# A transposing transfer in place of TensorE turns for the features of a graph-attention layer

## The reference, cut to what matters

```python
def _gat_layer(h, mask, b):
    scores = jnp.einsum('...nd,...md->...nm', h, h)
    scores = jnp.where(mask, scores, NEG)
    attn = jax.nn.softmax(scores, axis=-1)
    return jnp.einsum('...nm,...md->...nd', attn, h) + b
...
h = jnp.einsum('bnc,hdc->bhnd', x, Wh)
out_h = _gat_layer(h, mask[None, None], bh[None, :, None, :])
...
h2 = jnp.einsum('bnk,dk->bnd', z, Wo)
out2 = _gat_layer(h2, mask[None], bo)
```

## Time and profile before

| | us |
|---|---|
| median of 3 runs (lowest, highest) | 1996.86 (1995.81, 1998.15) |
| the profiled execution | 1996.86 |
| its span in the profile | 1995.1 |
| PE matmul busy | 1904.9 (95%) |
| DVE busy | 1623.2 (81%) |
| ACT busy | 1243.6 (62%) |
| POOL busy | 1013.7 (51%) |
| FA transfers, 640 of 64 KB, issue to landing | 2.0 (median) |

### The profile page before, as it was taken

How to read it: one execution, slowest core, us unless ns; L and a number is a source line. 1 busy time by engine, 2 the same in 40 slices (tenths; PEclk the granted TensorE clock), 3 DMA queues, 4 the chain that set the end, 5 groups by cost and what they waited for, 6 DMA issues and landing times.

```text
span 1995.1 us, 95063 instructions
## 1 busy us (share of the span) xinstructions
PE 1904.9 (95%) x43624; PEld 1563.2 (78%) x43624; DVE 1623.2 (81%) x1975; ACT 1243.6 (62%) x1886; POOL 1013.7 (51%) x742
## 2 busy tenths in 40 slices
PE   8998899999999999999999999999999999989998
PEld 6787799977777777777777777777777777767887
DVE  6999999567787878778787878788778877767998
ACT  5887676246666666666666666666666666654342
POOL 6676899432345444444544444553445454253653
PEclk7999999999999999999999999999999999999999
DMA  7000000011111111111111111111111111101111
GB/s 182 4 4 4 3 2 3 2 34 35 35 34 34 32 33 33 30 35 34 35 35 32 35 28 35 33 34 35 34 34 29 34 31 33 35 13 25 25 25 35
DMA packets 88255, 61.24 MB, mean 31 GB/s; under 512 B 45616, under 2 KB 86832, under 8 KB 87856
## 3 DMA queue, kind: packets, MB, share of 16 engines
q1 hardware_dynamic: 85632, 54.57, 11.2%
q10 hardware_dynamic: 2224, 0.59, 0.1%
HBM read 8.98 MB, written 4.19 MB: 7 GB/s over the span
## 4 chain that ended last, share of the span: by engine, by line
PE 69%; DVE 15%; ACT 5%; POOL 5%; issue 2%; DMA 2%; SPq 1%; ACTq 0%; POOLq 0%; DVEq 0%
PE ACC L1638 29%; PE S L1819 22%; PE S L1798 8%; DVE ring L1412 6%; PE AX L1862 3%; DVE ring L1266 2%; PE AX L1871 2%; PE AX L1839 2%; POOL sp_log L788 1%; POOL ln_sq L791 1%; DMA FA<-lo 1%; ACT ring L1066 1%; PE AX L1618 1%; DVE score L1421 1%; PE S L1695 1%
## 5 line engine op out<-in xcount | busy, mean ns | idle before, releaser
L1638 PEld LDWEIGHTS ACC<-V,ring 128*64 128x64 f32 x28672 | 953.5, 138 | 180.5 <-DVE ring L1266 34.0
L1412 DVE TENSOR_TENSOR ring<-ring,mask_self_t 128x1024 f32<-128x1024 f32 x640 | 822.1, 1287 | 270.0 <-ACT ring L1066 261.3
L1638 PE MATMUL ACC<-V,ring 128*64 128x65 f32 x28672 | 972.6, 223 | 29.7 <-DVE ring L1266 12.3
L1066 ACT ACTIVATE ring<-S,dot_bias 128x1024 f32<-128x1024 f32 x640 | 713.4, 1115 | 420.3 <-PE S L1819 384.4
L1819 PE MATMUL S<-FA 128*64 128x512 f16 x5120 | 666.5, 382 | 7.5 <-DMA FA<-lo 7.5
L1819 PEld LDWEIGHTS S<-FA 128*64 128x64 f16 x5120 | 253.3, 110 | 168.6 <-ACT ring L1066 15.9
L1266 DVE SCALAR_TENSOR_TENSOR ring<-S,pair_q,mask_t 128x1024 f32<-128x1024 f32 x256 | 315.1, 1272 | 15.1 <-DVE f_max L1278 4.6
L804 POOL TENSOR_TENSOR EV_both<-score,recip 128x512 f32<-128x512 f32 x64 | 115.4, 1803 | 222.3 <-DVE score L1421 222.2
L797 POOL TENSOR_TENSOR V<-v_pairs,bh_bc 128x512 f32<-128x512 f32 x64 | 95.4, 1490 | 164.9 <-ACT v_pairs L1086 164.9
L1798 PE MATMUL S<-parts,mask_t 128*128 128x128 bf16 x3072 | 172.0, 219 | 1.6 <-DVE o L1401 1.4
L1798 PEld LDWEIGHTS S<-parts,mask_t 128*128 128x128 bf16 x3072 | 171.6, 98 | 1.8 <-issue 1.8
(11 more groups left out here) (134 smaller groups left out, 2078.9 us busy)
## 6 DMA issues: line engine op xcount, KB each, us to landing
FA<-hi SPq DMA_DIRECT2D x320, 64.0 KB, 2.0
FA<-lo SPq DMA_DIRECT2D x320, 64.0 KB, 2.0
X<-in_x SPq DMA_DIRECT2D x16, 256.0 KB, 5.0
ring<-in_adj SPq DMA_DIRECT2D x8, 512.0 KB, 8.4
out_x<-X SPq DMA_DIRECT2D x16, 256.0 KB, 2.6
wh<-in_wh_t ACTq DMA_DIRECT2D x2, 64.0 KB, 6.5
bh_bc<-in_bh ACTq DMA_DIRECT2D x1, 128.0 KB, 9.7
w_gat<-in_w_gat ACTq DMA_DIRECT2D x4, 16.0 KB, 3.7
```

The source lines that it names most:

```text
L1066: act.activation(ring[:, jt, :], S[jt % 2][:, :], ACT.Exp, bias=dot_bias[:, n % 2:n % 2 + 1])\
L1412: dve.tensor_tensor(ring[:, jt, :], ring[:, jt, :], mask_self_t[:, jt, :], ALU.mult)\
L1638: last = pe.matmul(acc_of(t)[rows, :], ring[:, jt, t * P + c * CUT:t * P + (c + 1) * CUT], values, start=(jt == 0 and t % 4 == 0), stop=(j ...
```

## The change

The features are no longer turned by PE. ACT copies the high half straight from `v_pairs` (SBUF) into a new buffer HL, node-major: for each node 64 high and 64 low values side by side. DVE makes the low half from `v_pairs` and HL. SP then issues one transposing transfer of the whole of HL's buffer (128 partitions x 1024 columns) into FA[:, par, 0], waits for it (`stacked`), and issues two plain copies of 128 KB that exchange the halves into FA[:, par, 1]. The step "F" leaves the order of the AX banks. Heads 0 and 1 are turned after tile 7 of head 3 instead of tile 5 on PE, and copied after tile 7 instead of 6 on ACT. ACT waits for the low half of the unit before (`lo_made`) before it writes `v_pairs` anew, and for the transfer out of the same HL buffer before it writes there. In the last layer the rest of the last unit is made after tile 3, ahead of its norms, and not after tile 5.

```diff
-        hi = sb("hi", [P, 2, HALF], F16)
-        lo = sb("lo", [P, 2, HALF], F16)
+        HL = sb("HL", [P, 2, T, 2 * D], F16)
...
+        stacked = [sem("stacked0"), sem("stacked1")]
...
         def moved_by(u):
-            return 16 * 8 * (u["n"] // 2 + 1)
+            return 16 * 2 * (u["n"] // 2 + 1)
...
             for u in UNITS:
                 par = buf_of(u)
-                moved = features_in[par]
-                sp.wait_ge(hi_made, u["n"] + 1)
-                for half in range(2):
-                    cols_of = slice(half * HALF, (half + 1) * HALF)
-                    own = slice(half * D, (half + 1) * D)
-                    sp.dma_start(FA[0:D, par, 0, cols_of], hi[own, par, :]).then_inc(moved, 16)
-                    sp.dma_start(FA[D:P, par, 1, cols_of], hi[own, par, :]).then_inc(moved, 16)
                 sp.wait_ge(lo_made, u["n"] + 1)
-                for half in range(2):
-                    cols_of = slice(half * HALF, (half + 1) * HALF)
-                    own = slice(half * D, (half + 1) * D)
-                    sp.dma_start(FA[D:P, par, 0, cols_of], lo[own, par, :]).then_inc(moved, 16)
-                    sp.dma_start(FA[0:D, par, 1, cols_of], lo[own, par, :]).then_inc(moved, 16)
+                sp.dma_start_transpose(out=FA[:, par, 0, :].rearrange("p (t n) -> p t n", t=T),
+                                       in_=HL[:, par, :, :].rearrange("p t n -> p (t n)")).then_inc(stacked[par], 16)
+                sp.wait_ge(stacked[par], 16 * (u["n"] // 2 + 1))
+                sp.dma_start(FA[0:D, par, 1, :], FA[D:P, par, 0, :]).then_inc(features_in[par], 16)
+                sp.dma_start(FA[D:P, par, 1, :], FA[0:D, par, 0, :]).then_inc(features_in[par], 16)
...
                 wait(act, v_made, u["n"])
+                wait(act, lo_made, u["n"])
                 act.activation(v_pairs, V_FULL, ACT.Copy).then_inc(v_copied, 1)
...
             def features(u):
-                k, at = AX_AT["F", u["n"]]
-                act.wait_ge(ax_full[k], at + 1)
                 if u["n"] >= 2:
-                    act.wait_ge(features_in[buf_of(u)], moved_by(UNITS[u["n"] - 2]))
-                act.activation(hi[:, buf_of(u), :], AX[k][:, :], ACT.Copy).then_inc(hi_made, 1)
+                    act.wait_ge(stacked[buf_of(u)], 16 * (u["n"] // 2))
+                act.activation(halves_of(HL[:, buf_of(u), :, 0:D]), v_pairs, ACT.Copy).then_inc(hi_made, 1)
...
-                if jt == 6 and is_head(u, 3):
+                if jt == 7 and is_head(u, 3):
                     turned(b, 0)
...
             def feature_rest(u):
-                k, at = AX_AT["F", u["n"]]
                 par = buf_of(u)
                 dve.wait_ge(hi_made, u["n"] + 1)
-                dve.tensor_tensor(lo[:, par, :], AX[k][:, :], hi[:, par, :], ALU.subtract).then_inc(lo_made, 1)
-                dve.wait_ge(lo_made, u["n"] + 1)
-                dve.sem_inc(ax_free[k], 1)
+                dve.wait_ge(v_copied, u["n"] + 1)
+                dve.tensor_tensor(halves_of(HL[:, par, :, D:2 * D]), v_pairs, halves_of(HL[:, par, :, 0:D]), ALU.subtract)\
+                    .then_inc(lo_made, 1)
...
-            def features(u):
-                pe.wait_ge(v_copied, u["n"] + 1)
-                k = take_bank(AX_AT["F", u["n"]])
-                for q in range(T // 2):
-                    last = pe.transpose(AX[k][:, q * P:(q + 1) * P], v_by_pair[:, q * P:(q + 1) * P], ident[:, :])
-                last.then_inc(ax_full[k], 1)
...
-                if jt == LAG - 1 and after(u):
-                    features(after(u))
...
-                if jt == 5 and is_head(u, 3):
+                if jt == 7 and is_head(u, 3):
                     turn_heads(b, 0)
```

More of the change, by code:

```diff
@@ L404, in place_values @@
                 place(("V", u["n"], half), half)
-        def place_features(u):
-            place(("F", u["n"]), 1)
         def place_bound(u):
@@ L421, in gnn_stack @@
         place_values(UNITS[0])
-        place_features(UNITS[0])
         place_bound(UNITS[0])
@@ L426, in gnn_stack @@
                 place_values(after(u))
-                place_features(after(u))
                 place_bound(after(u))
@@ L448, in gnn_stack @@
         place_values(LAST)
-        place_features(LAST)
         place_bound(LAST)
@@ L1492, in features @@
             def features(u):
+                feature_rest(u)
                 norms(u)
-                feature_rest(u)
             def dot_layer():
@@ L1528, in last_layer @@
                     if jt == 3:
+                        feature_rest(LAST)
                         norms(LAST)
-                    if jt == 5:
-                        feature_rest(LAST)
                     if jt == 6:
@@ L1756, in last_layer @@
                         values(LAST)
-                    if jt == 2:
-                        features(LAST)
                     if jt == 4:
@@ L1900, in first_features @@
                 values(UNITS[0])
-                features(UNITS[0])
             def dot_layer():
```

## The result

The changed kernel takes 2138.07 us (median of 4 runs, 2132.28 to 2146.68), the kernel before 1996.34 us (1995.45 to 1998.15): a ratio of 1.071 [1.067, 1.075]. It is slower, as forecast and inside the range, but by 142 us and not by 21.

A forecast was written before the change was run, and what follows sets the result against it. PE, busy 95% of the span, was taken to set the pace. The new loop, 11.53 + 6.05 = 17.58 us against 17.28, adds 23 us over 78 units; 1996.9 + 23 - 2 = 2018 us, range 1955 to 2172.

The forecast's parts named there:

- start, low half, last leg: Loop from a unit's start over the next unit's low half and transfers to the next start: 17.58 us.
- last leg: From the low half's end until the features reach FA: 6.05 us, against 3.8 before.
- the wait for the maximum: PE's wait for the bound's maximum at the turning of heads, 22.7 us in all, was to vanish.
- 3.05: Transposing transfer, issue to landing, in us: the middle of 2.6 (stores of x) and 3.5 (quickest load of x).
- plain-priced: Rival: transposing transfer lands within 2.7 us, loop falls below 17.28; about 1983 us, or 1961 with punctual landings; chance 0.30.
- break-even of 2.75: Transposing transfer time in us at which the loop breaks even, the whole stretch after the low half being 5.75.
- the pieces do not go in series: Denies the rival that the transfer's eight blocks go one after another: landing after 6.8 us, total 2310; chance 0.09.
- I put both at nothing: High half on ACT and low half on DVE, now reading SBUF with the same shapes: no added time.
- the 11.53 us: Mean time from a unit's start to the end of the next unit's low half on DVE.
- the predicted 17.58: Unit length in us from the loop, 11.53 + 6.05, above PE's own 16.5 and against 17.28 before.
- where I took 0.3: Allowance in us a unit for late landings of the two transfers in series after the low half.
- near 1 us each, 60 to 100 us in all: New waits of PE's first dots on the copies within FA, expected in most units.

The follow-up runs named there:

- divide_late: Changed kernel with one wait added: POOL's division by the softmax sums starts only once the low half is made; 2074.57 us.
- filled: Changed kernel with 16 small identity matmuls on PE ahead of its wait for the features; 2112.27 us.
- late_filled: Changed kernel with both POOL's division held until the low half is made and 16 matmuls ahead of PE's wait for the features; 2080.73 us.
- halves_early: Changed kernel with ACT's high half one tile earlier, ahead of its sums copy, and DVE's low half one tile earlier, ahead of the epilogue; 1967.40 us.
- halves_first: halves_early with DVE's low half moved earlier still, after the mask of tile 1 and ahead of the norms; 1971.58 us.
- norms_first: Changed kernel with high half and ACT's sums copy earlier, and norms, then low half, both after the mask of tile 1; 1926.14 us.
- turn_alone: Kernel before with only the turning of heads 0 and 1 moved to after tile 7 on PE and ACT; 1977.45 us.

## Why the prediction was right in its mechanism and wrong in its size

**What held.** PE loses the turns and doesn't get faster by it, because a loop of "start, low half, last leg" takes PE's place. The waits are in every unit, the wait for the maximum is gone, and the transposing transfer lands in 3.1 us against 3.05. ACT and DVE's place in the order did not move. The rivals fell: the transfer is not plain-priced, since plain is 2.3 and it is over the break-even of 2.75; and the pieces do not go in series. At 3.05 it was 0.3 us over that break-even, so the sign of the forecast rested on a term whose bounds lay on both sides of it.

**The step that failed** is the cost of the low half, put at nothing without a reason on DVE's side: "High and low half now read SBUF, with the same shapes ... I put both at nothing", and with it the 11.53 us. It takes 1.53 us at the median and not 0.68. The unit came to 19.09 us, 1.51 over the predicted 17.58. 1.51 x 78 = 118 us, of a miss of 120. It divides like this:

- *The low half, 12.50 for 11.53: 0.97 us, 76 us of the miss.* Two causes. The subtraction waits for POOL (shown by divide_late: 0.85 us a unit, 63 us of the kernel, a part of it by fewer half-clock stretches, 11 instead of 25). The clock is the other: filled, with 18 stretches fewer, gains 26 us, or 1.4 us each, so by estimate all 25 are worth about 36 us, which is 0.46 us a unit. The two overlap, and the sum is more than the 0.97; with both taken away, in late_filled, lo is 11.42, close to the predicted 11.53. I had the warning in hand: the earlier trace rows hold a multiply that took 1.65 us beside POOL, and I read it only as something a waiting PE would give back. It was the price of two SBUF operands on DVE beside POOL, and the change gave the low half two such operands.
- *The last leg, 6.58 for 6.05: 0.53 us, 41 us.* (The prediction's terms add up to 6.03.) The two copies took 2.82 us together at their quickest, not 2.65: the second issue is half a us after the first, and the landing is 2.3 and not 2.1. That is 0.17. Late landings are the rest: mean 3.37 for the transposing transfer against 3.04, and 3.13 for the copies against 2.82, so 0.6 where I took 0.3. They add up in series, as I had said, and they are not rare: 21 of the 78 transposing transfers landed later than 3.34 us, each beside an instruction fetch.
- *PE's waits*, "near 1 us each, 60 to 100 us in all", were 2.0 us each and 159.0. That is the same miss seen from PE. I tied the clock to waits over 4 us; it fell behind waits from 2.0 us up.

The rule I had not weighed is in the Trainium skill, SBUF — State Buffer, section "SBUF: two separate sides": the port pair that DVE and GpSimd (POOL here) share is held by one of them at a time, and a DVE operation with both inputs in SBUF waits for the whole of a GpSimd instruction that reads SBUF and started first. The trace agrees: 1.53 us beside the division and 0.68 without it, and 0.68 before, beside the same division, with one operand in PSUM. It doesn't agree for every instruction: beside L826, 2.7 us long and reading SBUF, the low half took 0.68, and there the measurement decides. The Trainium skill, Advanced Engine Details and Errata, section "X-Bar Transpose (TRN2)", would have the transfer as fast as a regular one; here 3.1 stands against 2.3 us, and the measurement decides. The estimate of 10.5 us, worked out from the Trainium skill, VectorE: DVE Perf Modes, section "The three transpose paths", is over three times too long for eight blocks in one transfer, which landed in 3.1; no run here has a single block.

**What the expectation of a gain misses.** The 55 us that left PE could not come in, because the next unit's features were already nearly late. And once the halves are made early, two other things are waited for that had no row of waits before: ACT's copy of the sums (14.9 us in halves_early, where the high half stands ahead of it) and DVE's norms (17.9 us in halves_first, where the low half stands ahead of them). Whether the turns had hidden the copy of the sums, as the expectations say, or only its new place made it late, no run tells apart. With halves, sums and norms in the order of norms_first PE sets the pace again: 16.35 us a unit, against 16.5 in the prediction for PE's own work. The kernel takes 51 us less than turn_alone, and PE's busy time in the window is 42 us less (1271.06 against 1313.56); the rest is idle time. What the order alone would give a kernel with turns is not shown.

## What to carry to other kernels

Before taking work off the busiest engine, measure the loop behind it: how long before its use each input is ready, and which transfers come in series after it; a change that shortens the engine and lengthens the loop loses twice, since the waits can also bring the clock down. When an edit moves an operand from PSUM to SBUF, look at what POOL runs at that moment; the shape says nothing about it. A transfer in place of engine work can pay when its source is made a few us earlier, as here; what then waits next has to be given its place again, here the sums and the norms.

## What the runs showed of the hardware

- A DVE subtraction of two 128x512 f32 and f16 tiles in SBUF takes 683 ns alone and 1531 ns (median) beside POOL's division of 128x512 f32 in SBUF, ending about 0.55 us after it; with one input in PSUM it takes 683 ns beside the same division (longest of 80: 692). Its time alone is that of divide_late. Beside POOL's power of 128x8 it takes 683 to 689 ns even with both in SBUF.
- A transposing transfer of 256 KB within SBUF in packets of 256 bytes lands 3.0 us after its issue at the least, a plain one of the same bytes in packets of 2048 bytes in 2.3; its issue takes 1.23 us of SP's queue, against 0.46 to 0.60 for the copies within FA.
- Landings of small transfers have a tail, up to 4.7 us for the transposing transfer and 4.3 for a copy. Two in series cost 0.6 us a unit on average here. Without an instruction fetch under way none landed later than 3.10 and 2.33 us in the changed kernel.
- Waits of PE of 2.0 us on average, up to 4.0, one every 19 us, brought 25 stretches, 92 us in all, at the 1.2 GHz level in 78 units; with 26 waits of 0.9 us on average (halves_early) the window's clock was 1.00.
